# Seventeen instead of eighteen of every 28 edge columns selected on TensorE in a four-layer graph network, and eleven gathers instead of ten

## The chip, the cores and the metric

The program runs on one core of one Trainium2 chip. The metric is the device time of one execution, in microseconds (us); shorter is better. A repeated measurement of this kernel can tell a change of about 0.2% from none.

## What is computed

Four graph layers over N = 6250 nodes and E = 200000 edges, sorted by destination, 16 features a node. Every layer fetches the features of each edge's source node, turns them into a message and reduces the messages of a destination:

```python
def layer0(x):  return segment_sum(tanh(x[src] * edge_weight[:, None]), dst)
def layer1(x):  # attention per edge, 16x16 logits and values, softmax over a destination's edges
    e1 = (efeat @ W_msg + b_msg).reshape(E, 16, 16) * x[src][:, :, None]
    e2 = (efeat @ W_attn + b_attn).reshape(E, 16, 16) * x[src][:, :, None]
    return segment_sum(e1 * segment_softmax(e2, dst), dst).sum(axis=1)
def layer2(x):  return segment_max(x[src] * edge_weight1, dst) @ W.T + b
def layer3(x):  # twice: h = relu(((1 + eps) * x + segment_sum(x[src], dst)) @ wa + ba) @ wb + bb
x = layernorm(x + layer(x))   # after each of the four
```

## The kernel before

The edges lie in a grid of 128 partitions by K = 1568 columns. Layer 1 is the attention stage (groups of G = 4 columns). The other reductions are four **narrow passes**: pass 0 (layer 0), then, after the attention stage, passes 1 (layer 2, a maximum), 2 and 3 (the two sums of layer 3). A narrow pass works through 56 groups of U = 28 columns, on two sets of buffers (s = 0 and 1) in turn, so a loop iteration is two groups; there are 4 x 56 = 224 groups. Only the source's features have to be fetched for a column (128 edges), and it is done in one of two ways:

- A = U - R = 10 columns are **gathered** by GpSimd (POOL): one indirect DMA a column, line 441, into `msg`. The first gather of a group waits for the indices `cidx`, which ScalarE copies out when the last gather of the group two back has landed (line 633). Gather u waits for the u-th signal `pick` that TensorE gives in the same group (`pick` comes A times, evenly over the group's matmuls).
- R = 18 columns are **selected on TensorE**. A source is node = 7 * quotient + remainder on one of 128 partitions. VectorE builds one-hot matrices `hot` for the seven quotients a column can have (`one_hots`, line 1029: seven instructions over R * 128 = 2304 elements, into `wide_buf` for s = 0 and `flat` for s = 1), and TensorE multiplies them with the node features, which are split into three bf16 parts (`fetch`, line 760): 7 x 3 = 21 matmuls of 112 moving columns for every edge column, 378 a group. The seven candidates of each edge then lie side by side in PSUM; VectorE masks them (`pick`, line 875 by way of the helper `tt`, PSUM to `raw`) and sums them into `msg` (line 1045).

PSUM has eight banks, and a bank holds four columns' blocks. Each set has three banks of its own for the first OWN = 12 columns. The other columns go into two banks that both sets use (`shared`), three columns in each; TensorE waits at column 12 until VectorE has read them out for the group before (`s_share`).

In every group VectorE goes: the one-hots of the next group, the masks `amask`, wait for the group's last matmul, three masking instructions out of PSUM (two shared banks, then the twelve own columns), the sum (line 1045), a copy of the reset row, the multiplication by the edge weight (passes 0 and 1), in pass 0 a wait for ScalarE's tanh, sixteen scans (line 1066), and in pass 0's first 50 groups one count over a gathered slice of destinations (line 1072). TensorE starts on a group when its one-hots are there and its own banks have been read; SP loads the quotients (`quot`) and stores `run`.

```python
def one_hots(j, s, first):
    ...
    for m in range(Q):
        last = v.tensor_scalar(hot[s][:, m, :], quot[:, s, :], count[:, 0, m:m + 1], None, ALU.is_equal)
```

Of the kernel before, what the change touches and what calls it, by code (L numbers as in the profile page):

```python
# [21 lines left out]
P = 128  # L22
N, E, D = 6250, 200000, 16
U = 28
R = 18
OWN = 12
A = U - R
G = 4
K = -(-E // (P * 2 * U)) * 2 * U
NB = -(-(N + 1) // P)  # L30
# [13 lines left out]
Q = 7  # L44
QW = Q * D
DW = DC * D
NCH = NB // DC
PB = 4
# [7 lines left out]
assert NB % 2 == 1 and SL < NG // 2 and NB % DC == 0 and K % (2 * G) == 0 and NG % 2 == 0 and 2 * G == 8  # L56
CONT, BOTH, CONT_NEG, BOTH_NEG = range(4)

assert NB == Q * Q and PB * QW <= 512 and OWN == 3 * PB and (R - OWN) % 2 == 0 and R - OWN <= 2 * PB and K % DW == 0

FP = mybir.dt.float32
BF = mybir.dt.bfloat16
# [2 lines left out]
ALU = mybir.AluOpType  # L65
# [4 lines left out]
def gnn_program(nc, x, src_in, dst_in, ew_in, ew1_in, ef_in, att_w, ident, dense_w, biases, eps, out):  # L70
# [5 lines left out]
    def sb(name, shape, dt=FP):  # L76
        return es.enter_context(nc.sbuf_tensor(name, shape, dt))
# [10 lines left out]
    with es:  # L88
# [56 lines left out]
        parts = sb("parts", [P, NB, 3, D], BF)  # L145
        amask = sb("amask", [P, R, Q])
        tailT = sb("tailT", [D, P])
# [12 lines left out]
        aring = sb("aring", [P, 2, 2, G])  # L160
        raw = sb("raw", [P, R * P + R * QW])
        wide_buf = sb("wide_buf", [P, Q * R * P // 2])
        amax_room = sb("amax_room", [P, 2 * DC * DD])
# [6 lines left out]
        wts = z_room[:, 0:K]  # L170
        flat = sb("flat", [P, Q * R * P // 2])
        st = flat[:, 0:2 * G * TW].rearrange("p (a g c) -> p a g c", a=2, g=G)
# [11 lines left out]
        picked = raw[:, R * P:R * P + R * QW].rearrange("p (r q c) -> p r q c", q=Q, c=D)  # L184
# [33 lines left out]
        msgs = [ps[:, s * G:(s + 1) * G, DD:2 * DD] for s in range(2)]  # L218
        mine_banks = [ps[:, 4 * s + 1:4 * s + 4, :].rearrange("p b (t c) -> p (b t) c", c=P) for s in range(2)]
        shared = [ps[:, 4 * h, :].rearrange("p (t c) -> p t c", c=P) for h in range(2)]  # L220
        SH = (R - OWN) // 2


        s_list = sem("s_list")
# [77 lines left out]
        block = es.enter_context(nc.Block())  # L302
# [416 lines left out]
        def _(pe):  # L719
# [25 lines left out]
            def narrow_pass(n):  # L745

                q, done = narrow, n * HALF
                pe.wait_ge(s_parts, n + 1)

                def fetch(j, s, first):  # L750
                    pe.wait_ge(q["hot"][s], done + j + 1)
                    if not first:
                        pe.wait_ge(q["read"][s], done + j)
                    for t in range(R):
                        if t == OWN and not (first and s == 0):
                            pe.wait_ge(s_share, n * NG + 2 * j + s)
                        block = mine_banks[s][:, t, :] if t < OWN else shared[(t - OWN) // SH][:, (t - OWN) % SH, :]
                        for m in range(Q):
                            for part in range(3):
                                last = nc.tensor.matmul(  # L760
                                    block[:, 0:QW].rearrange("p (q c) -> p q c", c=D),
                                    hot[s][:, m, t * P:(t + 1) * P], parts[:, m * Q:(m + 1) * Q, part, :],
                                    start=m == 0 and part == 0, stop=m == Q - 1 and part == 2)
                                done_now = t * 3 * Q + 3 * m + part + 1
                                if done_now * A // (R * 3 * Q) > (done_now - 1) * A // (R * 3 * Q):
                                    last.then_inc(q["pick"][s], 1)

                if n == 0:
                    for s in range(2):
                        fetch(0, s, True)  # L770
                with pe.Fori(1 if n == 0 else 0, HALF) as j:
                    for s in range(2):
                        fetch(j, s, False)
# [13 lines left out]
            for c in range(K // DW):  # L787
                last = nc.tensor.transpose(ps[0:DW, c // PB, (c % PB) * P:(c % PB + 1) * P], quotf[:, c * DW:(c + 1) * DW], idm[:])
# [56 lines left out]
        def _(dve):  # L845
# [14 lines left out]
            def hold(ins):  # L860

                looped[0] += 1
                ins.then_inc(s_loop, 1)
                dve.wait_ge(s_loop, looped[0])
# [9 lines left out]
            def tt(dest, a, b, op):  # L874
                return v.tensor_tensor(dest, a, b, op)  # L875
# [104 lines left out]
            for b in range(4):  # L980
                chunks = min(PB, K // DW - b * PB)
                last = v.tensor_copy(quotT[0:DW, b * PB:b * PB + chunks, :],
                                     ps[0:DW, b, 0:chunks * P].rearrange("p (c q) -> p c q", q=P))
# [34 lines left out]
            def narrow_pass(n):  # L1018
                q, done = narrow, n * HALF
# [12 lines left out]
                def pick(j, s):  # L1032

                    hold(tt(amask[:], rem[:, bass.ds((2 * j + s) * U + A, R)].unsqueeze(2).to_broadcast([P, R, Q]),
                            count[:, 1, :].unsqueeze(1).to_broadcast([P, R, Q]), ALU.is_equal))
                    dve.wait_ge(q["pick"][s], (done + j + 1) * A)
                    for h in range(2):
                        lo, hi = OWN + h * SH, OWN + (h + 1) * SH
                        last = tt(picked[:, lo:hi], shared[h][:, 0:SH, 0:QW].rearrange("p r (q c) -> p r q c", c=D),
                                  amask[:, lo:hi].unsqueeze(3).to_broadcast([P, SH, Q, D]), ALU.mult)  # L1040
                    last.then_inc(s_share, 1)
                    tt(picked[:, 0:OWN], mine_banks[s][:, :, 0:QW].rearrange("p r (q c) -> p r q c", c=D),
                       amask[:, 0:OWN].unsqueeze(3).to_broadcast([P, OWN, Q, D]), ALU.mult).then_inc(q["read"][s], 1)
                    dve.wait_ge(q["read"][s], done + j + 1)
                    hold(v.tensor_reduce(msg[:, s, A:U, :], picked.rearrange("p r q c -> p r c q"), AX.X, ALU.add))  # L1045

                def round_(j, more, first, slice_=False, next_=False):
                    loop_start()
                    for s in range(2):
                        g = 2 * j + s  # L1050
                        if more or s == 0:
                            one_hots(j + s, 1 - s, first and s == 0)
                        pick(j, s)
                        hold(v.tensor_copy(mring[:, s, :], mask[:, bass.ds(g * U, U)]))
                        dve.wait_ge(q["got"][s], (done + j + 1) * (16 * A))
                        values = msg
                        if n < 2:
                            tt(val[:, s], msg[:, s], wts[:, bass.ds(g * U, U)].unsqueeze(2).to_broadcast([P, U, D]),
                               ALU.mult).then_inc(q["mul"][s], 1)
                            values = val  # L1060

                            dve.wait_ge(q["act"][s] if n == 0 else q["mul"][s], done + j + 1)
                        if not first:
                            dve.wait_ge(q["put"][s], 16 * (done + j))
                        for c in range(D):
                            last = v.tensor_tensor_scan(run[:, s, :, c], mring[:, s, :], values[:, s, :, c], run[:, 1 - s, U - 1, c:c + 1],  # L1066
                                                        ALU.add if most else ALU.mult, ALU.max if most else ALU.add)
                        last.then_inc(q["run"][s], 1)
                        dve.wait_ge(q["run"][s], done + j + 1)
                        if slice_:  # L1070
                            dve.wait_ge(s_slice[s], 16 * (j + 1))
                            hold(v.tensor_scalar(junk[:], slices[:, s, :], nid[:, bass.ds(g, 1)], 0.0, ALU.is_le, ALU.add,
                                                 accum_out=cle[:, bass.ds(g, 1)]))
                            if next_:
                                next_slice(g + 2, s)
# [328 lines left out]
```

## Time and profile before

| | |
|---|---|
| time, median of 3 runs | 9269.36 us (9264.99 to 9275.45) |
| span of the profiled execution | 9349.5 us |
| TensorE (matmuls) busy | 7169.2 us, 77% |
| VectorE busy | 7190.8 us, 77% |
| GpSimd busy | 5015.4 us, 54% |
| matmuls of line 760 | 84672 |

The profile gives no device time of its own for the profiled execution beside its span; the span is 80 us, 0.9%, above the median of the runs without the profiler. Of the span, pass 0 takes up to about 1280 us, the attention stage runs to about 5400 us, and passes 1 to 3 fill the rest, with short stretches between them. A matmul's busy time overlaps that of its neighbours, so a stretch of them is read by its length and count.

### The profile page before, as it was taken

How to read it: one execution, taken by the hardware profiler on the slowest of the kernel's cores; microseconds unless marked ns; L12 is line 12 of the kernel's file. 1: busy time of each engine (PE TensorE's matmuls, PEld its weight loads, DVE VectorE, ACT ScalarE, POOL GpSimd, SP SyncE). 2: the span in 40 equal slices, each digit the busy share in tenths (PEclk: the TensorE clock that was granted, in tenths of full speed). 3: DMA queues.
4: the chain of work that ended last, by engine and by line, in shares of the span. 5: the costliest groups of instructions: out<-in, count | busy, mean ns of one | idle time of the engine just before them, and what ended most of it. 6: DMA issues, size and time to landing. Idle time of an engine off the chain costs nothing.

```text
span 9349.5 us, 249505 instructions
## 1 busy us (share of the span) xinstructions
PE 7169.2 (77%) x98927; PEld 6793.7 (73%) x98927; DVE 7190.8 (77%) x14062; ACT 1830.3 (20%) x4253; POOL 5015.4 (54%) x4569
## 2 busy tenths in 40 slices
PE   6999946777777677776667709999869999599995
PEld 6888846666666666666666609999769999599994
DVE  7778848888888888888888857777657777477774
ACT  0000004444444444444444420000000000000000
POOL 3555555555555555555555554555444555445554
PEclk9999978777777877777887759999989999799997
DMA  2222214444444444444444421111111111111111
GB/s 88 79 78 80 80 21 123 123 123 123 123 119 122 123 123 123 120 121 123 123 123 123 120 85 42 46 43 46 35 38 43 46 43 46 27 43 46 45 43 23
DMA packets 794677, 758.23 MB, mean 81 GB/s; under 512 B 210208, under 2 KB 754784, under 8 KB 794560
## 3 DMA queue, kind: packets, MB, share of 16 engines
q1 hardware_dynamic: 649088, 668.17, 22.1%
q0 software_dynamic: 140528, 86.77, 6.0%
q10 hardware_dynamic: 5008, 2.59, 0.1%
q8 instruction: 32, 0.52, 0.0%
q14 instruction: 21, 0.17, 0.0%
HBM read 240.60 MB, written 519.73 MB: 81 GB/s over the span
## 4 chain that ended last, share of the span: by engine, by line
PE 59%; DVE 19%; issue 14%; ACT 3%; POOL 3%; DMA 1%; DVEq 1%; ACTq 0%; another core or an unknown queue 0%; SPq 0%; POOLq 0%
PE ps L760 43%; PE ps L811 9%; PE ps L804 6%; DVE amax_room L1139 4%; DVE flat L1171 3%; DVE spare L1144 3%; DVE flat L875 2%; POOL got L441 2%; DVE ps L875 2%; DVE stt L875 2%; ACT wide_buf L671 1%; ACT ps L672 1%; POOL wide_buf L441 1%; ACT aring L677 1%; DVE msg L1045 0%
## 5 line engine op out<-in xcount | busy, mean ns | idle before, releaser
L441 POOL DMA_INDIRECT msg<-feat,cidx x1680 | 1722.4, 1025 | 1781.3 <-PE ps L760 1422.6
L760 PE MATMUL ps<-parts,wide_buf 128*128 128x112 bf16 x42336 | 2184.8, 213 | 418.6 <-DVE wide_buf L1029 271.9
L760 PEld LDWEIGHTS ps<-parts,wide_buf 128*128 128x128 bf16 x42336 | 2111.5, 98 | 481.6 <-issue 477.0
L441 POOL DMA_INDIRECT hsrc<-feat,aidx x1568 | 1537.4, 981 | 1626.4 <-DMA aidx<-src_sorted 1236.0
L760 PE MATMUL ps<-parts,flat 128*128 128x112 bf16 x42336 | 2170.0, 213 | 116.9 <-issue 107.4
L760 PEld LDWEIGHTS ps<-parts,flat 128*128 128x128 bf16 x42336 | 2098.4, 98 | 175.7 <-issue 172.6
L804 PE MATMUL ps<-idm,z_room 128*102 128x128 f32 x4704 | 1113.3, 362 | 1274.6 <-DVE flat L875 1030.7
L811 PE MATMUL ps<-wsb,zT 102*128 102x192 f32 (+1 forms) x9408 | 2038.5, 371 | 13.0 <-ACT zT L665 10.4
L811 PEld LDWEIGHTS ps<-wsb,zT 102*128 102x128 f32 x9408 | 1954.2, 243 | 21.6 <-ACT zT L665 13.9
L804 PEld LDWEIGHTS ps<-idm,z_room 128*102 128x102 f32 x4704 | 680.1, 168 | 1513.7 <-issue 659.6
L875 DVE TENSOR_TENSOR raw<-ps,amask 128x336 f32<-128x336 f32 (+1 forms) x672 | 534.7, 851 | 996.3 <-remote 476.0
L665 ACT ACTIVATE zT<-ps 102x384 f32<-102x384 f32 x1568 | 770.1, 491 | 2334.9 <-PE ps L804 2019.0
L1139 DVE SCALAR_TENSOR_TENSOR amax_room<-amax_room,aring,ps 128x256 f32<-128x256 f32 x1568 | 746.9, 476 | 281.3 <-ACT aring L677 238.0
L441 POOL DMA_INDIRECT msg<-in_x,cidx x560 | 576.4, 1029 | 628.8 <-PE ps L760 405.6
L1171 DVE SCALAR_TENSOR_TENSOR flat<-flat,aring,ps 128x512 f32<-128x512 f32 x1176 | 872.4, 742 | 0.1
L633 ACT ACTIVATE cidx<-sidx 128x10 int32 (+1 forms) x224 | 46.8, 211 | 4076.7 <-DMA msg<-feat,cidx 3287.6
L502 POOL TENSOR_TENSOR z_room<-efs,hsrc 128x1088 f32<-128x1088 f32 x392 | 813.2, 2074 | 47.6 <-DVE spare L1152 28.6
L1045 DVE TENSOR_REDUCE msg<-raw 128x288 f32<-128x2016 f32 x224 | 815.1, 3639 | 7.7
L875 DVE TENSOR_TENSOR ps<-ps,wide_buf 128x512 f32<-128x512 f32 x784 | 545.0, 695 | 213.7 <-ACT ps L672 180.7
L1029 DVE TENSOR_SCALAR flat<-raw,count 128x2304 bf16<-128x2304 f16 x784 | 582.8, 816 | 74.3 <-DVE run L1066 50.0
L1029 DVE TENSOR_SCALAR wide_buf<-raw,count 128x2304 bf16<-128x2304 f16 x784 | 585.5, 817 | 20.1 <-DVE run L1066 11.6
L672 ACT ACTIVATE ps<-ps 128x512 f32<-128x512 f32 x784 | 470.7, 600 | 0.0
(210 smaller groups left out, 4274.0 us busy)
## 6 DMA issues: line engine op xcount, KB each, us to landing
state_tab<-flat SPq DMA_DIRECT2D x784, 512.0 KB
raw<-quot_tab SPq DMA_DIRECT2D x224, 576.0 KB
run_tab<-run SPq DMA_DIRECT2D x224, 224.0 KB
top_tab<-spare SPq DMA_DIRECT2D x392, 128.0 KB
msg<-feat,cidx POOLq DMA_INDIRECT x1680
hsrc<-feat,aidx POOLq DMA_INDIRECT x1568
efs<-in_ef SPq DMA_DIRECT2D x392, 34.0 KB, 1.9
msg<-in_x,cidx POOLq DMA_INDIRECT x560
```

The source lines that it names most:

```text
L441: return pool.indirect_dma_start(dest, None, table, rows_at(idx))
L502: nc.gpsimd.tensor_tensor(z[:, s].rearrange("p g (i f) -> p g i f", f=F), efs[:, s].rearrange("p (g f) -> p g f", f=F).unsqueeze(2).to_bro ...
L665: nc.scalar.activation(zT[0:CW, 3 * k:3 * k + 3, :], ps[0:CW, s * G + k, 0:3 * P].rearrange("p (c q) -> p c q", q=P), ACT.Copy).then_inc(a ...
L672: nc.scalar.activation(logits[s][:, lo:hi, :], logits[s][:, lo:hi, :], ACT.Exp).then_inc(a_exp[s], 1)
L760: last = nc.tensor.matmul(block[:, 0:QW].rearrange("p (q c) -> p q c", c=D), hot[s][:, m, t * P:(t + 1) * P], parts[:, m * Q:(m + 1) * Q, ...
L804: last = nc.tensor.transpose(ps[0:CW, s * G + k, c * P:(c + 1) * P], z[:, s, k, FROM[c] * F:FROM[c] * F + CW], idm[:])
L811: last = nc.tensor.matmul(ps[:, s * G + k, :].rearrange("p (t i o) -> p i t o", t=2, o=D)[:, NEW[c]:NEW[c + 1]], zT[0:CW, 3 * k + c, :], w ...
L875: return v.tensor_tensor(dest, a, b, op)
L1029: last = v.tensor_scalar(hot[s][:, m, :], quot[:, s, :], count[:, 0, m:m + 1], None, ALU.is_equal)
L1045: hold(v.tensor_reduce(msg[:, s, A:U, :], picked.rearrange("p r q c -> p r c q"), AX.X, ALU.add))
L1139: return mark(v.scalar_tensor_tensor(amax[:, s, k, :], amax[:, 1 - s, G - 1, :] if k == 0 else amax[:, s, k - 1, :], aring[:, s, 0, k:k + ...
L1171: out = v.scalar_tensor_tensor(st[:, s, k, :], st[:, s, k - 1, :], aring[:, s, 1, k:k + 1], bank, ALU.mult, ALU.add)
```

## The change

R goes from 18 to 17, so A = U - R goes from 10 to 11: one column of every group goes over from TensorE to a gather. The five columns past the twelfth now lie three in the first shared bank and two in the second; a tuple `SHARED` holds the bounds for TensorE and VectorE. Nothing else is edited; everything that is sized by R or A follows: 357 matmuls a group, eleven `pick` signals, one-hots of 2176 elements, the quotients' load.

```diff
-R = 18
+R = 17
...
-        SH = (R - OWN) // 2
+        SHARED = (OWN, OWN + (R - OWN + 1) // 2, R)
...
                         if t == OWN and not (first and s == 0):
                             pe.wait_ge(s_share, n * NG + 2 * j + s)
-                        block = mine_banks[s][:, t, :] if t < OWN else shared[(t - OWN) // SH][:, (t - OWN) % SH, :]
+                        h = int(t >= SHARED[1])
+                        block = mine_banks[s][:, t, :] if t < OWN else shared[h][:, t - SHARED[h], :]
...
                     for h in range(2):
-                        lo, hi = OWN + h * SH, OWN + (h + 1) * SH
-                        last = tt(picked[:, lo:hi], shared[h][:, 0:SH, 0:QW].rearrange("p r (q c) -> p r q c", c=D),
-                                  amask[:, lo:hi].unsqueeze(3).to_broadcast([P, SH, Q, D]), ALU.mult)
+                        lo, hi = SHARED[h], SHARED[h + 1]
+                        last = tt(picked[:, lo:hi], shared[h][:, 0:hi - lo, 0:QW].rearrange("p r (q c) -> p r q c", c=D),
+                                  amask[:, lo:hi].unsqueeze(3).to_broadcast([P, hi - lo, Q, D]), ALU.mult)
```

TensorE's loop over pass 0 (the two groups that are written out, then the loop of two groups; lines after the change are one higher):

```order
-L760 MATMUL ps<-parts,wide_buf 128x112 x378
-L760 MATMUL ps<-parts,flat 128x112 x378
...
-L760 MATMUL ps<-parts,wide_buf 128x112 x252
+L761 MATMUL ps<-parts,wide_buf 128x112 x357
+L761 MATMUL ps<-parts,flat 128x112 x357
...
+L761 MATMUL ps<-parts,wide_buf 128x112 x252
 L756 REGISTER_ALU
-L760 MATMUL ps<-parts,wide_buf 128x112 x126
-L760 MATMUL ps<-parts,flat 128x112 x252
+L761 MATMUL ps<-parts,wide_buf 128x112 x105
+L761 MATMUL ps<-parts,flat 128x112 x252
```

The twelve own columns keep their 252 matmuls; behind the wait for the shared banks (line 756) 105 follow instead of 126.

GpSimd's queue in pass 0: the first groups with their slice gathers (`amax_room`), and the end of the loop body of the rest:

```order
-L441 DMA msg<-in_x,cidx 128x16 x10
-L441 DMA amax_room<-dst_sorted,pring 128x1568
-L441 DMA msg<-in_x,cidx 128x16 x10
+L441 DMA msg<-in_x,cidx 128x16 x11
+L441 DMA amax_room<-dst_sorted,pring 128x1568
+L441 DMA msg<-in_x,cidx 128x16 x11
...
-L441 DMA msg<-in_x,cidx 128x16 x11
+L441 DMA msg<-in_x,cidx 128x16
+L458 REGISTER_ALU
+L441 DMA msg<-in_x,cidx 128x16 x12
```

Every group has one gather more, and one more wait for `pick` ahead of it.

## Rows read from the trace of the kernel before

**Rows 1.** The page: busy us by engine; a group: busy us, mean ns | idle before

```profile
PE 7169.2 (77%) x98927; PEld 6793.7 (73%) x98927; DVE 7190.8 (77%) x14062; ACT 1830.3 (20%) x4253; POOL 5015.4 (54%) x4569
...
L760 PE MATMUL ps<-parts,flat 128*128 128x112 bf16 x42336 | 2170.0, 213 | 116.9 <-issue 107.4
```

**Rows 2.** Windows of passes 0, 1 and 3: us, then busy us of each engine, TensorE's granted clock, DMA share, GB/s

```profile
77.00:1290.00 1213.00, 1096.85 (x21170) 1055.29 (x21170) 947.37 (x1832) 45.00 (x111) 625.24 (x611) 0.99 0.26 74
5620.00:6765.00 1145.00, 1068.55 (x21070) 1041.10 (x21067) 840.37 (x1669) 11.40 (x54) 580.91 (x564) 0.99 0.16 43
8110.00:9255.00 1145.00, 1065.06 (x21039) 1039.42 (x21036) 807.23 (x1613) 11.40 (x54) 576.97 (x565) 0.99 0.16 43
```

**Rows 3.** The once-a-group sum, line 1045, of each pass: duration min/median/max, first and last start

```profile
L1045 DVE TENSOR_REDUCE msg<-raw x56: 3559/3630/3667, 101.0 to 1274.1; 128x288 f32<-128x2016 f32 x56
L1045 DVE TENSOR_REDUCE msg<-raw x56: 3562/3645/3669, 5638.5 to 6745.0; 128x288 f32<-128x2016 f32 x56
L1045 DVE TENSOR_REDUCE msg<-raw x56: 3556/3642/3672, 6876.3 to 7990.2; 128x288 f32<-128x2016 f32 x56
L1045 DVE TENSOR_REDUCE msg<-raw x56: 3557/3645/3659, 8126.8 to 9233.5; 128x288 f32<-128x2016 f32 x56
```

**Rows 4.** Timeline, one group of pass 1 (`flat`): start us, us, engine, [idle before <-releaser]

```profile
6601.52 11.69 PE L760 MATMUL ps<-parts,flat 128*128 128x112 bf16 x229
...
6601.72 2.39 DVE L875 TENSOR_TENSOR raw<-ps,amask 128x336 f32<-128x336 f32 x3 [2.56 <-PE ps L760]
...
6612.19 5.20 DVE L1029 TENSOR_SCALAR wide_buf<-raw,count 128x2304 bf16<-128x2304 f16 x7 [0.20 <-DVE run L1066]
...
6613.65 7.49 PE L760 MATMUL ps<-parts,flat 128*128 128x112 bf16 x149 [0.44 <-issue]
...
6616.36 1.15 POOL L441 DMA_INDIRECT msg<-feat,cidx  x1 [0.31 <-issue]
6617.31 0.29 DVE L875 TENSOR_TENSOR amask<-rem,count 128x126 f32<-128x126 f32 x1
...
6620.59 0.95 POOL L441 DMA_INDIRECT msg<-feat,cidx  x1 [1.14 <-PE ps L760]
...
6620.97 2.18 PE L760 MATMUL ps<-parts,wide_buf 128*128 128x112 bf16 x41
...
6621.84 0.95 POOL L441 DMA_INDIRECT msg<-feat,cidx  x1 [0.30 <-issue]
...
6623.13 0.21 ACT L633 ACTIVATE cidx<-sidx 128x10 int32 x1 [19.27 <-DMA msg<-feat,cidx]
...
6627.82 0.62 DVE L875 TENSOR_TENSOR val<-msg,z_room 128x448 f32<-128x448 f32 x1
```

**Rows 5.** Who waited for whom, the whole span: us in total, times, longest us

```profile
POOL msg L441 <- PE ps L760: 1828.1, 1272, 12.3
PE ps L760 <- issue: 249.7, 686, 1.1
```

**Rows 6.** Timeline, an unbroken piece of matmuls of pass 1

```profile
6642.88 7.29 PE L760 MATMUL ps<-parts,flat 128*128 128x112 bf16 x145 [0.32 <-issue]
```

**Rows 7.** Masking out of PSUM and gathers of pass 1: duration ns min/median/max

```profile
L875 DVE TENSOR_TENSOR raw<-ps,amask x24: 497/508/1549, 6601.7 to 6743.5; 128x336 f32<-128x336 f32 x16, 128x1344 f32<-128x1344 f32 x8
L441 POOL DMA_INDIRECT msg<-feat,cidx x548: 942/947/1775, 5640.2 to 6740.8; - x183
```

**Rows 8.** Timeline, VectorE in a group of pass 0 that counts a slice

```profile
615.52 2.39 DVE L875 TENSOR_TENSOR raw<-ps,amask 128x336 f32<-128x336 f32 x3
...
633.88 0.28 DVE L875 TENSOR_TENSOR amask<-rem,count 128x126 f32<-128x126 f32 x1
```

**Rows 9.** Windows: TensorE at half clock in pass 0, before it, the attention stage; columns as rows 2

```profile
422.30:425.70 3.40, 3.31 (x36) 3.30 (x36) 3.08 (x4) 0.00 (x0) 0.47 (x1) 0.50 0.34 137
418.70:422.30 3.60, 1.76 (x23) 1.12 (x21) 0.00 (x0) 0.21 (x1) 2.22 (x3) 1.00 0.41 98
1420.00:5390.00 3970.00, 2783.50 (x13958) 2538.22 (x13957) 3502.29 (x6984) 1674.08 (x3878) 2315.15 (x1930) 0.80 0.41 122
```

More of the change, by code:

```diff
@@ L57 @@
 CONT, BOTH, CONT_NEG, BOTH_NEG = range(4)
-assert NB == Q * Q and PB * QW <= 512 and OWN == 3 * PB and (R - OWN) % 2 == 0 and R - OWN <= 2 * PB and K % DW == 0
+assert NB == Q * Q and PB * QW <= 512 and OWN == 3 * PB and R - OWN <= 2 * PB and K % DW == 0
 FP = mybir.dt.float32
```

## The prediction

> **What bounds the kernel now.** I read the page first: TensorE and VectorE are both busy for 77% of the span [rows 1], which decides nothing, since the attention stage fills either in its own way and is not touched. So I took windows over the narrow passes. There TensorE is busy 1069 of 1145 us in pass 1 and 1097 of 1213 us in pass 0, at a granted clock of 0.99 (of 2.4 GHz), VectorE 840 and 947 us, GpSimd 581 and 625 us [rows 2]. TensorE is the fullest. Whether it is also the one that is waited for shows in the timeline of a group [rows 4]: the matmuls of `flat` run from 6601.5 to 6621.0 us and those of `wide_buf` follow at once; the one-hots for them were ready at 6617.4 us, and VectorE, its masks done at 6617.6 us, idles for almost 4 us until TensorE has ended the group. GpSimd waits for TensorE 1272 times, 1828 us in all [rows 5]. Nothing of consequence waits the other way: what TensorE's matmuls of line 760 wait for in the steady passes is "issue", 686 times, 249.7 us [rows 5].
>
> How long a group takes comes from the sum of line 1045, which runs once in it. From first to last start there are 55 groups: (1274.1 - 101.0) / 55 = 21.33 us in pass 0, and 20.12, 20.25 and 20.12 us in passes 1 to 3 [rows 3]. Over 56 groups each that is 56 x 81.82 = 4582 us of the span of 9349.5 us.
>
> A group's time has two parts. An unbroken piece of 145 matmuls lasts 7.29 us [rows 6], and one matmul lasts 0.213 us [rows 1], so they follow each other at (7.29 - 0.213) / 144 = 49.15 ns. The 84672 matmuls at that step are 4162 us; the other 420 us, 1.9 us a group, are **stalls**. A stall shows as 0.36 us of idle time on average (249.7 / 686) and costs 0.16 us more, because the row of a matmul (0.213 us) runs on past the step to the next one (0.049 us): 0.52 us, times 686 is 357 us, most of the 420.
>
> **The change, part by part.**
>
> *TensorE.* 21 matmuls fewer in each of 224 groups: 4704 x 49.15 ns = **-231 us**. All of it lies on the path, for the reason above. Here the Trainium skill has another price: its page "TensorE: Matmul & The Clock Gate", section "Back-to-back issue gap", gives a sustained step of about 81 ns for a weight load and a matmul of 128 columns, and says that its formula N / 2.4 + 2.5 ns counts too little at small N. By 81 ns the term would be -381 us. The trace disagrees: this stream has a weight load for each matmul and runs at 49.15 ns, which is what the formula gives for 112 columns. I take the row.
>
> *Stalls.* What they hang on is not in the trace, so I bound them from both sides. If they follow TensorE's own instructions, they fall by 1/18: -23 us. If each comes from a gather, they rise by a tenth: +42 us. For the second speaks that the one between the two pieces of rows 4 (6613.65 us) falls where gathers run at short intervals; against it, that only 686 of 2240 gathers have a stall. I take the middle, **+9 us**, and keep both ends for the range.
>
> *GpSimd.* One gather more a group. A gather takes 0.95 us in the median [rows 7] and the next can follow after 0.30 us [rows 4], so eleven need 11 x 1.25 = 13.8 us, and twelve with a slice 15 us, in a group of some 19 us. Cost: 0, covered by TensorE's own matmuls; if that cover were gone (a group under 13.8 us) each further gather would cost 1.25 us, 280 us in all. The wait that is added stands on GpSimd's queue ahead of the eleventh gather; behind it are the slice gather and the first gather of the next group. Before, the tenth gather, released by the ninth signal, starts at 6620.59 us, and ScalarE copies the next indices at 6623.13 us, when it has landed, 2.5 us later; VectorE needs the messages at 6627.82 us [rows 4], 4.7 us later still. After, the tenth of eleven signals releases the last gather, 1/11 of a group before its end (about 1.7 us) instead of 1/10 (2.0 us): 0.3 us of the 4.7 is used. The next group's first gather moves by as little. ScalarE's copy has one column more; it idles 19 us before it [rows 4].
>
> *VectorE.* The one-hots shrink by 1/18: between 0 and 0.29 us of 5.20 us [rows 4]; the sum likewise by up to 0.20 us of 3.64 us [rows 3]. The second masking instruction has 112 elements fewer; from 336 to 1344 elements costs 1549 - 508 ns [rows 7], so 1.03 ns an element, 0.12 us. It is 0.6 us of a group, hidden behind TensorE. It shows only at the ends: before a pass's first matmul are one-hots, after its last one the masking and the sum: 4 x 0.6 = **-2 us**. That the last shared bank holds two blocks instead of three changes no wait: TensorE comes to column 12 more than 12 us into the group (252 x 49.15 ns), VectorE has read the banks in the first 1.2 us.
>
> *DMA.* The quotients' load shrinks by 1/18, the eleventh gather moves 128 x 64 bytes; the queues are at 16% to 26% [rows 2]. Cost 0.
>
> **Sum:** -231 + 9 - 2 = -224 us: 9349.5 becomes about 9125 us of profiled span. The median of the runs, 9269.4 us, is 0.9% under that span; the same share of -224 us is -222 us, so I predict **9047 us** (-2.4%). A group should go from 20.1 to about 19.2 us.
>
> **The rivals.**
>
> A. *VectorE sets the pace in the part of pass 0 that counts slices* (50 groups). There its work runs from 615.52 to 634.16 us, 18.6 us, without a real pause [rows 8]; after the change it needs 18.0 us, and TensorE 21.33 - 1.03 = 20.3 us on average. For it: the margin shrinks, and a group with few stalls (17.5 us of matmuls) is shorter than VectorE's work. Against it: on average 2.3 us remain. If those groups gained only VectorE's 0.61 us instead of 1.03 us, 50 x 0.42 = 21 us are lost: 9068 us.
>
> B. *The gathers' stalls eat the gain* (slower). Place: in TensorE's stream, behind each of the now eleven releases, which come every 1.7 us instead of every 2.0 us. Price: 0.52 us a stall; today 686 of 2240 gathers have one, 31%. The point of decision: 233 / 0.52 = 448 stalls more, that is 1134 of 2464 gathers, 46%. At every second gather it would be 1232 stalls, +284 - 233 = +51 us: 9320 us. Such clusters can also pull the clock: after one (1.76 us of matmuls in 3.6 us) TensorE stood at half clock, 1.2 GHz, for 3.4 us and did 36 matmuls in place of 69 [rows 9], another 1.6 us; in the attention stage, with its broken stream, the granted clock is 0.80 [rows 9]. Against it: the dense stream of the passes keeps 0.99, and a share of 31% would have to rise by half from a spacing that is 0.3 us shorter.
>
> C. *The gathers set the pace and nothing is gained.* They would need 20.2 / 11 = 1.83 us each. The row against it is 1.25 us; for it, that one beside the one-hots took 1.15 instead of 0.95 us [rows 4] and the longest 1.78 us [rows 7]. Then 9269 us. The Trainium skill's "SBUF — State Buffer", section "Who interferes with whom", says that VectorE in its two-port modes locks GpSimd out for a whole instruction. By that rule four gathers a group could each wait out a one-hot instruction of 0.74 us, 13.8 + 3 = 16.8 us, still under TensorE; the trace shows delays of 0.2 us.
>
> D. *The stalls fall with the matmuls*, and TensorE's time shrinks by a full 1/18: -231 - 23 - 2 = -256 us: 9013 us.
>
> **How the numbers follow.** My forecast has 0.74, A 0.12, D 0.08, B 0.04, C 0.02. The range takes in D below and, above, A with the gathers' full stall price (9269 - 233 + 42 + 21 = 9099 us): 9008 to 9099 us. B and C, 0.06, stay outside, with some of the forecast's own spread. A measurement tells about 0.2% (19 us) from no change. Faster by more than that: forecast, A and D, 0.94; within it: C, 0.02; slower: B, 0.04.
>
> **What would show it.** 79968 matmuls of line 761, at the same 49 ns step; the once-a-group sum at 20.2 to 20.4 us in pass 0 and 19.1 to 19.3 us in passes 1 to 3; VectorE still idle ahead of the masking; the clock at 0.99. Right on the stalls: between 660 and 760 of them. Wrong: a group of 19.5 us or more in passes 1 to 3 (then the number of stalls tells whether it is B), "PE <- DVE" among the long waits (A), or GpSimd without waits for TensorE (C). If the attention stage moves by more than a few us, something that I have not considered has changed.

## The result

| | us, median | ratio to the kernel before, 95% interval |
|---|---|---|
| before | 9267.2 (4 runs, 9264.7 to 9275.5) | |
| changed | 9351.8 (4 runs, 9344.7 to 9358.0) | 1.009 (1.0078 to 1.0103) |
| forecast | 9047 (9008 to 9099) | 0.976 |

The changed kernel is 0.9% slower where I had forecast 2.4% faster. The experiments then showed the same kernel at 0.9764 (0.9748 to 0.9781) of the kernel before on another chip. Both are right: on some chips TensorE's stream has stalls that it doesn't have on others, and the change makes them more.

First the trace that belongs to the first result. The page of the changed kernel, against [rows 1]:

```profile
PE 7073.7 (76%) x94223; PEld 6608.3 (71%) x94223; DVE 7060.0 (76%) x14062; ACT 1833.0 (20%) x4253; POOL 5207.8 (56%) x4793
```

4704 matmuls are gone and 224 gathers have come, as intended. The sum that runs once a group, in the four passes, against [rows 3]:

```profile
L1046 DVE TENSOR_REDUCE msg<-raw x56: 3353/3404/3456, 100.5 to 1293.0; 128x272 f32<-128x1904 f32 x56
L1046 DVE TENSOR_REDUCE msg<-raw x56: 3353/3431/3454, 5657.5 to 6760.4; 128x272 f32<-128x1904 f32 x56
L1046 DVE TENSOR_REDUCE msg<-raw x56: 3354/3427/3459, 6889.7 to 7994.2; 128x272 f32<-128x1904 f32 x56
L1046 DVE TENSOR_REDUCE msg<-raw x56: 3353/3434/3454, 8128.4 to 9232.9; 128x272 f32<-128x1904 f32 x56
```

Over 55 groups each that is 21.68, 20.05, 20.08 and 20.08 us, where [rows 3] gave 21.33, 20.12, 20.25 and 20.12 us: nothing was gained, with 21 matmuls fewer in each group. The four passes take 56 x 81.89 = 4586 us; 79968 matmuls at 49.15 ns are 3930 us of it, and 656 us are stalls, where they were 420 ("stalls" is here all time beyond the step, whatever its cause). Who waited for whom says the same (us in total, times, longest), against [rows 5]:

```profile
POOL msg L441 <- PE ps L761: 1477.2, 1041, 11.0
...
PE ps L761 <- issue: 342.8, 969, 1.2
```

969 stalls in place of 686. One caution: the two spans are equal (9348.5 and 9349.5 us), while the runs differ by 84 us. The execution traced of the kernel before was longer than any of its runs here, and it is not on record on which chip it ran, so the traces show the change too favourably; what they show of the stalls' places is used below, and a difference in time only with that reserve.

**Where the stalls stand.** I took from both traces every start-to-start distance of two gathers in pass 1 (from 5640 to 6740 us, distances under 4 us) and asked whether TensorE stalled (a matmul starts more than 0.13 us behind the one before) 0.75 to 1.5 us after the second gather's start:

```
distance of two gathers   before: number, with a stall   changed: number, with a stall
1.20 to 1.40 us           116, 96%                       252, 92%
1.40 to 1.60 us            68, 74%                        67, 55%
1.60 to 1.80 us            25,  8%                        16,  0%
over 1.80 us              328,  0%                       263,  0%
```

So a stall does not come with a gather but with a gather that starts **close** behind another, under 1.6 us. Pass 0, with its slice gathers counted too, says the same (under 1.4 us 167 of 181 before and 291 of 308 changed; over 1.8 us 1 of 330 and 2 of 285). And nearly all stalls of pass 1 lie there: 83 of 84 us before, and all 132 us changed, fall 0.2 to 2.3 us behind the start of a close gather, which is 0.45 and 0.41 us for each of 185 and 319 close gathers (counted between the first and last sum of the pass). These stretches cover at most 35% and 61% of the pass.

The timeline of GpSimd in the changed kernel, pass 1 (start, us, operation, [idle before <-releaser]):

```profile
6345.86 0.98 POOL L441 DMA_INDIRECT msg<-feat,cidx  x1 [1.39 <-PE ps L761]
6347.14 0.99 POOL L441 DMA_INDIRECT msg<-feat,cidx  x1 [0.30 <-issue]
6349.43 1.04 POOL L441 DMA_INDIRECT msg<-feat,cidx  x1 [1.30 <-PE ps L761]
6350.78 1.08 POOL L441 DMA_INDIRECT msg<-feat,cidx  x1 [0.30 <-issue]
6352.99 0.96 POOL L441 DMA_INDIRECT msg<-feat,cidx  x1 [1.13 <-PE ps L761]
6354.26 0.94 POOL L441 DMA_INDIRECT msg<-feat,cidx  x1 [0.31 <-issue]
```

A gather that waited for its signal, then one 1.3 us behind it whose signal was there already, and so on: every second one is close. With signals 1.86 us apart (378 matmuls in ten) most gathers could keep their distance; with 1.6 us (357 in eleven) they can't. The stall itself moves the next signal back by half a microsecond, which may keep the pairs going (not shown). That reading was formed after the result, so it had to be tested.

### The profile page after: what moved, and what is told of

Read it like the earlier page. It is cut to its first block, busy times and chain, and to the rows that moved or that the text cites. A ratio compares the mean times of both kernels' runs of the same rounds, so it can differ in the third digit from the quotient of the medians.

```text
span 9348.5 us, 240656 instructions
## 1 busy us (share of the span) xinstructions
PE 7073.7 (76%) x94223; PEld 6608.3 (71%) x94223; DVE 7060.0 (76%) x14062; ACT 1833.0 (20%) x4253; POOL 5207.8 (56%) x4793
## 4 chain that ended last, share of the span: by engine, by line
PE 65%; DVE 15%; issue 12%; POOL 3%; ACT 3%; DMA 1%; DVEq 0%; ACTq 0%; POOLq 0%; SPq 0%
PE ps L761 45%; PE ps L812 11%; PE ps L805 8%; DVE amax_room L1140 4%; DVE flat L1172 3%; DVE spare L1145 2%; DVE flat L876 2%; POOL got L441 2%; DVE stt L876 2%; DVE ps L876 1%; ACT wide_buf L671 1%; ACT ps L672 1%; ACT aring L677 1%; POOL wide_buf L441 1%; ACT spare L674 0%
## 5 line engine op out<-in xcount | busy, mean ns | idle before, releaser
L441 POOL DMA_INDIRECT msg<-feat,cidx x1848 | 1853.4, 1003 | 1631.4 <-PE ps L761 1109.5
L761 PE MATMUL ps<-parts,wide_buf 128*128 128x112 bf16 x39984 | 2134.9, 214 | 475.9 <-DVE wide_buf L1030 267.9
L761 PEld LDWEIGHTS ps<-parts,wide_buf 128*128 128x128 bf16 x39984 | 2023.9, 99 | 578.7 <-issue 568.9
L761 PE MATMUL ps<-parts,flat 128*128 128x112 bf16 x39984 | 2113.9, 213 | 159.6 <-issue 143.7
L761 PEld LDWEIGHTS ps<-parts,flat 128*128 128x128 bf16 x39984 | 2006.0, 98 | 254.8 <-issue 244.4
L876 DVE TENSOR_TENSOR raw<-ps,amask 128x336 f32<-128x336 f32 (+2 forms) x672 | 508.4, 811 | 1123.7 <-PE ps L761 579.5
L633 ACT ACTIVATE cidx<-sidx 128x11 int32 (+1 forms) x224 | 47.1, 212 | 4125.5 <-DMA msg<-feat,cidx 3274.1
L1046 DVE TENSOR_REDUCE msg<-raw 128x272 f32<-128x1904 f32 x224 | 766.9, 3424 | 7.7
L1030 DVE TENSOR_SCALAR flat<-raw,count 128x2176 bf16<-128x2176 f16 x784 | 557.5, 782 | 74.3 <-DVE run L1067 56.6
L1030 DVE TENSOR_SCALAR wide_buf<-raw,count 128x2176 bf16<-128x2176 f16 x784 | 557.8, 783 | 19.6 <-DVE run L1067 14.7
```

The source lines that it names most:

```text
L441: return pool.indirect_dma_start(dest, None, table, rows_at(idx))
L761: last = nc.tensor.matmul(block[:, 0:QW].rearrange("p (q c) -> p q c", c=D), hot[s][:, m, t * P:(t + 1) * P], parts[:, m * Q:(m + 1) * Q, ...
```

## The experiments

All runs are compared with runs of the kernel before on the same chip. They went to ten chips. On eight of them the kernel before took 8950 to 8954 us, on one 9265 us, on one 9368 us. The chip of the first result is not on record; its 9267 us match those of the chip with 9265 us. Each of the ten was visited once, so what is called a property of the chip below could also belong to how the program lay on it that time; runs on one chip agree.

**1. The kernel before again.** No edit.

> The kernel before, unchanged, to have a trace of it from the same chip as the runs below. Its time should be 9265 to 9280 us. The trace before and the trace after have the same span (9349.5 and 9348.5 us) though the runs differ by 84 us, so either this profile shows a span near 9270 us and fewer than 686 TensorE stalls (then the first trace was of a longer execution), or again near 9350 us (then the profiler itself adds to the kernel before).

8955 us (its companions 8952 us, 13 runs). The difference from 9267 us is in the stalls: the sum of line 1045 from 101.4 to 1140.2 us in pass 0 gives 18.89 us a group. Passes 1 to 3 have no gap of over 0.13 us between matmuls at all, though 81 to 84 gathers of each are close, and pass 0 has 45 such gaps, 16 us, none behind a close gather. A group of pass 1 is 18.59 us, which is 378 x 49.15 ns = 18.58 us. The table above is one of a chip, then, as much as of a kernel. The difference lies in the four passes alone: the attention stage, from the last sum of pass 0 to the first of pass 1, takes 4364.4 us in the first trace and 4365.5 us in this one.

**2. Columns and gathers apart.** Two theories stood: S, a gather stalls TensorE when it is close behind another; N, every gather costs the same. First 17 columns with ten gathers:

```diff
+GA = A - 1
-                        for u in range(A):
+                        for u in range(GA):
```

(signals, waits and counts follow GA; the last gathered column is left out and its message is zero.) Then 18 columns with eleven gathers:

```diff
-R = 17
+R = 18
+GA = A + 1
-                            gather(msg[:, s, u, :], table, cidx[:, s, u:u + 1]).then_inc(q["got"][s], 16)
+                            gather(msg[:, s, u, :] if u < A else spare_msg[:, s, :], ...).then_inc(q["got"][s], 16)
```

> 17 columns on TensorE, but only ten gathers a group (the eleventh is left out, its message is zero). Theory S (spacing): TensorE stalls about 0.45 us when two gathers start less than 1.6 us apart, and never when they are 2 us apart; a gather that has to wait for its signal starts 2.2 us after the one before, one whose signal is already there 1.25 us after, so the number c of close ones follows from 2.2(n-c) + 1.25c = group = matmuls + 0.45c. For n = 10 and 17.55 us of matmuls: c = 3.2, group 19.0 us, 0.7 us less than the kernel before by the same formula, so about 9110 us. Theory N (number: every gather costs the same 0.2 us of stall wherever it stands): 9267 - 231 = 9036 us.

> 18 columns on TensorE and eleven gathers (the last one is done twice, the second time into a tile that nobody reads). Theory S: c = 4.0, group 0.7 us longer than the kernel before: about 9420 us. Theory N: one gather more at 0.2 us, 224 times: 9267 + 45 = 9312 us.

8742.7 us (0.9765, 0.9749 to 0.9781) and 8952.1 us (0.9999, 0.9990 to 1.0009), on the chip without stalls. Neither theory's number is met, since both suppose stalls; neither run tests them. What they do show: where nothing stalls, a gather more costs nothing and a column less on TensorE gives 209 us. The kernel with 17 columns and ten gathers ran once more, on a further such chip, and took 8739.8 us (0.9764).

> 17 columns on TensorE, ten gathers (the eleventh left out). Kernel before near 8952 us: 8743 us. Kernel before near 9267 us: theory S about 9110 us (the formula of spacing), theory N (a fixed 0.2 us a gather) 9036 us.

**3. No waits between gathers.**

```diff
                         for u in range(A):
-                            if u:
-                                pool.wait_ge(q["pick"][s], (done + j) * A + u)
-                                pool.sem_inc(s_pool, 1)
```

> The changed kernel without the waits for TensorE's signals between the gathers, so that they follow each other at 1.25 us. Theory S: ten of eleven gathers of a group are close, 10 x 0.45 = 4.5 us of stalls a group in place of some 2.5 us: about 9350 + 400 = 9750 us. Theory N, or a theory that the waits themselves do the harm: no slower than 9350 us.

8743.2 us (0.9761, 0.9745 to 0.9778): on this chip 539 of 594 distances of gathers in pass 1 are now under 1.6 us, and still no stall follows.

**4. The change itself on two chips.** Theory E: the stalls go with where the program runs. Theory K: they belong to the changed kernel.

> The changed kernel, unedited. On the chip of the first four runs the kernel before took 8952 us instead of 9267 us and TensorE had next to none of the short stalls behind close gathers that both first traces show. If the stalls are a property of where the program runs (theory E), then on a chip without them the change gives its full 231 us, about 8742 us (ratio 0.976), and on a chip with them it is again about 1.009. If they belong to the changed kernel itself (theory K), the ratio is 1.009 on any chip.

> The changed kernel, unedited. Theory E (the stalls go with the chip): where the kernel before takes 8952 us, this takes 8742 us, ratio 0.976; where the kernel before takes 9267 us, 9350 us, ratio 1.009. Theory K (the changed kernel stalls on any chip): ratio 1.009.

9349.3 us against 9265.2 us (1.0086, 1.0069 to 1.0103) on the first, 8741.9 us against 8952.8 us (0.9764, 0.9748 to 0.9781) on the second, one kernel file. Theory K falls; the stalls go with where the program runs. Windows of pass 1 of the changed kernel, in the trace of the first result and on the second of these chips (columns as [rows 2]):

```profile
5640.00:6740.00 1100.00, 1020.84 (x19596) 975.92 (x19594) 790.92 (x1623) 11.46 (x54) 602.68 (x604) 1.00 0.17 43
```

```profile
5450.00:6420.00 970.00, 970.00 (x19725) 970.00 (x19723) 796.50 (x1627) 11.46 (x54) 614.52 (x608) 1.00 0.20 48
```

On the second TensorE is busy without a gap. Both have the full granted clock there, so the difference in pass 1 is not the clock.

**5. Memsets in place of the waits**, to keep the gathers 1.6 us apart.

```diff
+                    pool.sem_clear(s_idle)
...
                             if u:
-                                pool.wait_ge(q["pick"][s], (done + j) * A + u)
-                                pool.sem_inc(s_pool, 1)
+                                idled = s * (A - 1) + u
+                                if idled > 1:
+                                    pool.wait_ge(s_idle, idled - 1)
+                                nc.gpsimd.memset(idle[:, 0:320], 0.0).then_inc(s_idle, 1)
...
+                    pool.wait_ge(s_idle, 2 * (A - 1))
```

(each memset waits for the one before it; the tile `idle` and its semaphore are new.)

> The changed kernel with the waits for TensorE's signals between gathers replaced by a GpSimd memset of 320 elements, so that gathers stand about 1.6 us apart whatever TensorE does. Theory S (close gathers stall TensorE, where the chip has such stalls at all): the stalls of a group fall from ten or more a group of some 0.25 to 0.45 us to at most two or three, and the time to about 9267 - 231 - 200 = 8850 to 8950 us on a chip with stalls; on a chip without them no different from the changed kernel, about 8742 us. Rival F (the stalls are TensorE's own instruction fetch, and only fall in step with the gathers): no gain over the changed kernel on either.

9857.1 us (1.0635, 1.0618 to 1.0653) on the chip where the kernel before takes 9265 us: a clear miss. The timeline shows why it tests less than I meant:

```profile
6313.65 0.39 POOL L464 MEMSET idle<- 128x320 f32 x1
...
6314.20 0.95 POOL L443 DMA_INDIRECT msg<-feat,cidx  x1 [0.17 <-issue]
6315.15 0.39 POOL L464 MEMSET idle<- 128x320 f32 x1
...
6315.70 0.95 POOL L443 DMA_INDIRECT msg<-feat,cidx  x1 [0.17 <-issue]
```

Here the gathers stand 1.50 us apart, not 1.6, which is inside the distance that stalls, and there is no longer a wait that opens a gap of 2.3 us now and then. In pass 1 339 distances are between 1.4 and 1.6 us, 193 between 1.6 and 1.8 us and 62 longer; of the 193 two have a stall behind them, of the 62 none. Its waits name the stalls:

```profile
PE ps L767 <- issue: 576.5, 1786, 1.1
```

1786 stalls in place of 969. Distance alone doesn't give that: there are 339 close gathers in pass 1 where the changed kernel has 319, but each has 0.62 us of stalls, not 0.41. What raises it, the unbroken row of close gathers or the memsets beside them, was not separated. The same file on a chip without stalls:

> The kernel with memsets between the gathers, which took 9857 us where the kernel before took 9265 us. Where the kernel before takes 8952 us: if the memsets themselves (GpSimd at 1.5 us a gather and one-hots lengthened from 5.0 to 6.3 us) made the kernel slow, it is far above 8742 us here too; if nearly all of the 9857 us were TensorE stalls, it is within 1% of 8742 us, since eleven gathers at 1.5 to 1.8 us are 16.5 to 19 us a group. I expect 8780 us.

8814.7 us (0.9847, 0.9831 to 0.9863). So the memsets themselves cost 73 us against 8742 us, in pass 0, where a group goes from 18.27 to 19.49 us; passes 1 to 3 stay at 17.55 to 17.58 us. The other 435 us of the loss against 9349 us come only with stalls: on that chip the gaps of over 0.13 us between matmuls hold 995 us in place of 597, and steps at half clock 160 us in place of 54.

**6. Is it the waits and signals rather than the distance?** In the runs so far a kernel with more GpSimd instructions always stalled more (theory Q). The kernel of 3 again, and with one signal a group from TensorE in place of eleven:

```diff
-                                if done_now * A // (R * 3 * Q) > (done_now - 1) * A // (R * 3 * Q):
+                                if done_now == R * 3 * Q:
```

(VectorE's waits follow.)

> The changed kernel without the waits between gathers once more, hoped for on a chip where the stalls exist (kernel before near 9267 us). There theory S (every gather that starts under 1.6 us behind another stalls TensorE by about 0.3 to 0.45 us) gives ten close gathers a group: 3 to 4.5 us of stalls in place of 2.6 to 2.9, so slower than the changed kernel, 9450 to 9750 us. Theory Q (the stalls go with the instructions and semaphore traffic of GpSimd's queue; a wait and an increment ahead of each gather add to it, as the memsets did in the 9857 us run): fewer stalls, below 9349 us. On a chip without stalls: 8743 us, as before.

> As the run before, and TensorE gives one signal a group instead of eleven. If the eleven increments by matmuls are part of the stalls, this is faster than the run before on a chip with stalls by 224 x 10 x a good share of 0.3 us (some 300 us or more); if the gathers alone make them (S), it is the same within 0.3%.

8743.7 and 8741.2 us (0.9767 and 0.9764), on a chip without stalls, so neither theory was tested. The kernel of 3 met four more such chips, at 8743.8, 8739.7, 8742.7 and 8742.7 us (0.9765 and 0.9766):

> As r7, which met a chip on which the kernel before takes 8952 us and nothing stalls: on a chip where it takes 9267 us, theory S says 9450 to 9750 us, theory Q below 9349 us.

> The changed kernel without the waits between gathers, again in search of a chip with the stalls. Kernel before near 8952 us: 8743 us. Kernel before near 9267 us: theory S (close gathers stall TensorE) 9450 to 9750 us; theory Q (GpSimd's waits and increments are part of it) below 9349 us.

> Kernel before near 8952 us: 8743 us. Kernel before near 9267 us: theory S 9450 to 9750 us; theory Q below 9349 us.

> Kernel before near 8952 us: 8743 us. Kernel before near 9267 us: theory S (close gathers stall TensorE) 9450 to 9750 us; theory Q (waits and signals do) below 9349 us.

The last run met a chip with stalls. It is the kernel before (18 columns, ten gathers) with the edit of 3:

> The kernel before with nothing changed but that the waits between its ten gathers are gone, so that all ten of a group are close. Where the kernel before takes 8952 us: the same, 8952 us, since a group stays at 378 x 49.15 ns = 18.6 us. Where it takes 9267 us: theory S gives nine close gathers in place of some 3.3, so up to 5.7 x 0.35 = 2 us a group more, about 9700 us; theory Q, that the waits and increments are part of the stalls, less than 9267 us.

11700.0 us against 9368.3 us on that chip: 1.2491 (1.2470 to 1.2512). The direction is theory S's, the size over five times what I had priced (2332 us, not the 433 from 9267 to 9700 us). Theory Q falls as far as it speaks of GpSimd's waits and increments: they were taken away and the stalls grew. Theory N falls with it: the gathers are as many as before, only closer. TensorE's ten signals a group are still in this kernel; the run without them, above, met no stalls either way, so their part was not tested. Its timeline (a group of pass 1):

```profile
7301.00 0.94 POOL L441 DMA_INDIRECT msg<-feat,cidx  x1 [0.30 <-issue]
...
7302.25 0.94 POOL L441 DMA_INDIRECT msg<-feat,cidx  x1 [0.30 <-issue]
7302.78 0.53 PE L758 MATMUL ps<-parts,wide_buf 128*128 128x112 bf16 x4 [0.90 <-issue]
...
7303.49 0.95 POOL L441 DMA_INDIRECT msg<-feat,cidx  x1 [0.30 <-issue]
...
7304.21 0.62 PE L758 MATMUL ps<-parts,wide_buf 128*128 128x112 bf16 x5 [0.89 <-issue]
...
7304.75 0.94 POOL L441 DMA_INDIRECT msg<-feat,cidx  x1 [0.30 <-issue]
...
7305.64 0.43 PE L758 MATMUL ps<-parts,wide_buf 128*128 128x112 bf16 x3 [0.81 <-issue]
...
7306.38 0.25 PE L758 MATMUL ps<-parts,wide_buf 128*128 128x112 bf16 x1 [0.30 <-issue]
...
7307.07 7.90 PE L758 MATMUL ps<-parts,wide_buf 128*128 128x112 bf16 x123 [0.44 <-issue]
...
7314.81 10.88 PE L758 MATMUL ps<-parts,flat 128*128 128x112 bf16 x218
```

While GpSimd issues a gather every 1.25 us, TensorE gets through three to five matmuls for each of them; when the last gather is out, it does 341 in one go. One burst of ten gathers costs a group some 12 us: it takes 30.2 to 30.5 us in passes 1 to 3. The broken stream also costs clock:

```profile
7000.00:8000.00 1000.00, 725.84 (x11845) 665.58 (x11843) 476.34 (x949) 6.10 (x29) 334.65 (x330) 0.82 0.11 27
```

The granted clock is 0.82 in this stretch, where pass 1 of the kernel before had 0.99. Over the passes the gaps between matmuls hold 2188 us and steps at half clock 568 us, together about the 2740 us by which this span exceeds that of the kernel before on a chip without stalls. A close gather costs more here the longer the row of close ones it stands in. In pass 1 they are mostly single in the first two traces, for 0.41 to 0.45 us of gaps each; two to four in a row in experiment 5, for 0.62 us each; nine in a row here, for 1.11 us each (536 us on 482). That these kernels also differ in other things, and in part in the chip, leaves it a reading and not a rule.

**7. Further columns to the gathers**, without waits, R = 16 and R = 15 (for 15 the buffers `wide_buf` and `flat` keep the 3584 x 2 elements that the attention stage needs).

> One column further: 16 on TensorE, twelve gathers, no waits between the gathers. On a chip without stalls (kernel before 8952 us) TensorE needs 336 x 49.15 ns = 16.5 us a group, GpSimd 12 x 1.25 = 15 us, VectorE some 15 to 16 us in passes 1 to 3 and 17.5 to 18 us in the slice part of pass 0, so the gain over 17 columns is about 1.0 us in passes 1 to 3 (-173 us) and little in pass 0 (-10 to -25 us): about 8550 us. On a chip with stalls (9267 us) theory S gives 16.5 + 11 x 0.35 = 20.4 us a group, about 9350 us or more; theory Q gives under 9200 us.

> 15 on TensorE, thirteen gathers, no waits between gathers. Where the kernel before takes 8952 us: GpSimd needs 13 x 1.25 to 1.3 = 16.3 to 16.9 us a group, more than TensorE's 15.5 us, and VectorE 15 us, so passes 1 to 3 stay at 16.3 to 16.9 us a group against 16.52 us at 16 columns, and pass 0 at VectorE's pace gains 0.4 us a group: 8500 to 8600 us, within 0.7% of the 8534 us of 16 columns. Where the kernel before takes 9267 us: theory S 15.5 + 12 x 0.35 = 19.7 us a group, theory Q under 9200 us.

8534.4 us (0.9534, 0.9518 to 0.9550) and 8489.7 us (0.9483, 0.9467 to 0.9499), both on chips without stalls; the first is 16 us below what I expected there, the second 10 us below its range. At R = 16 a group is 16.52 us in passes 1 to 3, at R = 15 it is 16.2 us, which is GpSimd's 13 x 1.25 us = 16.25 us, more than TensorE's 315 x 49.15 ns = 15.5 us: the turning point, by that estimate (no kernel beyond it was run). They beat both kernels by 2.4% to 5% there. On a chip with stalls they were not run; the run above, with ten gathers in a burst, suggests that they would lose there.

## Why the prediction was wrong, point by point

- **What bounds the kernel, and the term of -231 us: right.** The step of 49.15 ns held everywhere (18.59 and 17.55 us a group without stalls), and where nothing stalls nearly the whole term is there: the change gives 211 us of 8953 us. The rest went to rival A: pass 0 goes from 18.89 to 18.27 us a group, 0.62 and not 1.03 us, and the longest wait of TensorE for work is then for VectorE:

```profile
PE ps L761 <- DVE flat L1030: 19.2, 25, 0.9
```

  35 us from pass 0 and 168 x 1.03 = 173 us from the others are 208 us; the -2 us at the ends of the passes fit the rest.
- **The step that failed is the stall term, "I take the middle, +9 us", with its bounds of -23 and +42 us.** By the traces it was +236 us, by the difference of the runs (84 + 231 us) some +315 us. About 20 us of the latter are rival A's, which chips without stalls show as well: against the 8952 and 8742 us there, the stalls cost the kernel before 315 us and the changed one 610 us, so the term was +295 us. The upper bound took each gather to bring the same share of a stall, so that a tenth more gathers could bring a tenth more stalls. In truth a stall hangs on the distance of two gathers, and the number of close gathers in pass 1 goes from 185 to 319, by 72%, when the signals move from 1.86 to 1.6 us. The rows that I had chosen carried it: GpSimd's row with idle 0.30 <-issue at 6621.84 us [rows 4] is a close gather, and a stall follows 1.3 us behind it, where the `wide_buf` piece ends. I named "gathers at short intervals" as speaking for the upper bound, and did not count them. The other bound, that stalls follow TensorE's own instructions, has nothing for it either: 21 matmuls fewer a group brought more of them.
- **Rival B was the outcome**, in the very place and near the price named (0.5 us a stall; it was 0.41 to 0.46 us), and it had 0.04. Its sign, a group of 19.5 us or more in passes 1 to 3, came: 20.05 to 20.08 us. I held against it that the share of gathers with a stall would have to rise by half "from a spacing that is 0.3 us shorter"; by the waits it rose from 31% to 39% of all gathers. That is short of my point of decision of 46%, and yet the stall time of the trace grew by as much as the matmuls gave (236 against 231 us), because the waits don't count all stalls. The starts of the matmuls have 1446 gaps of over 0.13 us where the trace before has 876, which is 570 more (my point of decision was 448 more), with 599 us in place of 406; and 1135 steps take 0.08 to 0.10 us, half clock, where 298 did, for 50 us in place of 13. That is 230 of the 236 us. So the count of 686 that the term, its bounds and the point of decision start from was too low, and the half clock that B names as an extra did come, as a small part.
- **GpSimd at no cost, with an added wait: right where nothing stalls** (18 columns with eleven gathers, 0.9999), wrong elsewhere, because I looked at what the gather does to GpSimd's queue and not to what runs beside it.
- **Rival C** and the rule on VectorE's port played no part: GpSimd still waited for TensorE 1041 times.
- **The range** left B out; its two ends for the stall term were two guesses about one and the same assumption, that the number of gathers decides.

What stays open is the stall's physical cause. Neither the engine clock (1.00 in pass 1), nor VectorE (no wait for it in the steady groups), nor GpSimd's waits and increments (theory Q) make it; whether TensorE's signals have a part was not tested. That it comes with close gathers, and grows when they are made closer, is shown; what the two chips have that the eight don't is not. The gathers' own packets are no slower there: in pass 1 the median packet takes 39 to 44 ns in four traces with stalls and 41 to 46 ns in three without. TensorE's own instruction fetch was rival F of experiment 5, and that run, slower, does not refute it. The page shows hardly any fetched instructions, 0.5 MB over the whole span, and as many on a chip without stalls, so the loop is not read from memory anew each time as far as the profile records it:

```profile
q8 instruction: 30, 0.49, 0.0%
```

No run on a chip with stalls had all its gathers over 1.6 us apart, and so it was not tried how far apart, between 1.6 and 1.9 us, eleven gathers would have to stand for the change to win on a chip with stalls.

## What to carry to other kernels

Where one engine is paced by another's signals, look at the distances between its operations and not only at their number: a move that takes work off the busiest engine can push the paced one from regular steps into pairs. Before costing an edit, split the bound engine's time into steps and stalls, and ask of each stall what started a microsecond before it; that table of distances is cheap and might have turned this forecast: the formula of theory S, made after the result, gives 19.7 us a group for both kernels, which is no gain (20.05 to 20.25 us was measured for both). And time a change whose gain is a few per cent on more than one chip: here the same two files give 0.976 on one and 1.009 on another, and the pacing waits, which bring nothing on the chips without stalls, save the kernel before from 25% more time on a chip with them (11700 us against 9368 us).

## What the runs showed of the hardware that I had not expected

- Two chips of the ten slow a dense stream of matmuls behind close indirect DMAs of GpSimd by 0.4 to 0.5 us each, and in a burst to three to five matmuls per 1.25 us; the other eight show no stall even at 1.25 us. The kernel before takes 8952 us on the eight and 9265 and 9368 us on the two.
- The limit of distance is sharp on a chip with stalls: in pass 1 92 to 96% of gathers have a stall under 1.4 us, 55 to 74% between 1.4 and 1.6 us, none over 1.8 us.
- The Trainium skill's page "SBUF — State Buffer", section "Who interferes with whom", says that TensorE and ScalarE never wait on anyone. For the SBUF ports that may hold; TensorE's stream as a whole does stop behind GpSimd's DMAs here, on two chips, for 0.41 to 0.45 us a close gather. Through what it stops no run shows.
- On a chip without stalls 17 columns run at 970.00 us busy of 970 us: 357 pairs of weight load and matmul a group, 49.15 ns each, without a gap.
